# Reordering the statistics matmuls of one loop iteration on TensorE, in a fused LayerNorm, convolution and routing kernel

## The reference, cut to what matters

```python
x = x + conv(ln_c(x))          # ln_c: over the 64 channels; conv: group norm, 1x1 conv w1, relu, 1x1 conv w2, residual
t = tokens(x)                  # one token per pixel, 64 channels
t = t + ffn(ln_t(t))           # ffn: per image 32 experts choose 8 tokens each by a softmax of gate logits,
                               # expert MLP on the weighted sum of the 8, result added back to the 8 tokens
```

## Time and profile before

| what | us |
|---|---|
| median of 3 runs (lowest, highest) | 632.74 (632.73, 635.37) |
| time of the profiled execution | 639.6 |
| span of its trace | 637.9 |
| TensorE matmul busy | 535.4 |
| VectorE busy | 487.2 |
| ScalarE busy | 435.3 |

### The profile page before, as it was taken

One profiled execution on the slowest core, in us unless ns is written; L12 is line 12 of the kernel. 1 busy time (PEld: TensorE's weight loads), 2 busy tenths in 40 slices (PEclk: granted clock), 3 DMA queues, 4 the chain that ended last, 5 costly groups with the idle time before them and its releaser, 6 DMA issues.

```text
span 637.9 us, 14170 instructions
## 1 busy us (share of the span) xinstructions
PE 535.4 (84%) x5732; PEld 270.3 (42%) x5732; DVE 487.2 (76%) x950; ACT 435.3 (68%) x651; POOL 189.6 (30%) x116
## 2 busy tenths in 40 slices
PE   2749999898998899889989899989887988876982
PEld 1324444444444344444444444444443433434762
DVE  5574556689888988898789878988888687799620
ACT  2463779677976797679767976797677855984110
POOL 1007435023502260217020802080207145121144
PEclk9955999999999999999999999999998998987595
DMA  8960144714471447244634454445401255430000
GB/s 195 195 144 0 68 133 142 188 68 133 133 199 67 134 133 191 76 133 134 168 98 134 115 160 123 133 101 165 133 35 67 76 182 154 146 100 5 6 15 19
DMA packets 26752, 73.38 MB, mean 115 GB/s; under 512 B 4152, under 2 KB 4152, under 8 KB 22592
## 3 DMA queue, kind: packets, MB, share of 16 engines
q1 hardware_dynamic: 25664, 71.44, 40.9%
q0 software_dynamic: 1024, 1.05, 0.6%
HBM read 38.40 MB, written 34.08 MB: 114 GB/s over the span
## 4 chain that ended last, share of the span: by engine, by line
PE 41%; DVE 30%; ACT 13%; issue 12%; DMA 2%; POOL 1%; SPq 0%; ACTq 0%; DVEq 0%; POOLq 0%
PE st L372 11%; ACT junk L801 7%; DVE xs L948 7%; PE cv L383 6%; PE cv L391 6%; PE tl L400 6%; PE bc L494 5%; DVE us L938 5%; DVE lg L936 3%; DVE top_i L1035 2%; ACT tok L766 2%; DVE us L940 2%; DVE cnd L1030 2%; DMA xs<-in_x 2%; PE tl L409 2%
## 5 line engine op out<-in xcount | busy, mean ns | idle before, releaser
L1426 POOL TENSOR_TENSOR xs<-xs,us 128x1024 f32<-128x1024 f32 x64 | 151.2, 2379 | 367.2 <-DVE xs L948 173.4
L948 DVE SCALAR_TENSOR_TENSOR xs<-cv,vecs,xs 128x1024 f32<-128x1024 f32 x64 | 82.1, 1282 | 47.8 <-PE cv L391 47.7
L794 ACT ACTIVATE sqc<-us 128x1024 f32<-128x1024 f32 x64 | 67.5, 1054 | 46.2 <-DVE us L938 45.4
L761 ACT ACTIVATE hid<-cv,b1n 128x1024 f32<-128x1024 f32 x64 | 71.2, 1113 | 36.5 <-PE cv L383 36.0
L938 DVE TENSOR_TENSOR us<-xs,bc 128x1024 f32<-128x1024 f32 x60 | 73.0, 1216 | 19.7 <-PE bc L494 19.3
L400 PEld LDWEIGHTS tl<-ident,xs 128*128 128x128 f32 x512 | 63.8, 195 | 53.9 <-issue 53.9
L372 PE MATMUL st<-xs,stat_w 128*32 128x256 f32 x1024 | 74.5, 413 | 10.5 <-DMA xs<-in_x 9.4
L801 ACT ACTIVATE junk<-us 128x1024 bf16<-128x1024 f32 x64 | 67.3, 1051 | 22.8 <-DVE gsum L940 22.1
L940 DVE CUSTOM_DVE_ANT_0 us<-us,bc 128x1024 f32<-128x1024 f32 x60 | 72.9, 1215 | 11.2 <-PE bc L494 9.9
L400 PE MATMUL tl<-ident,xs 128*128 128x128 f32 x512 | 76.4, 294 | 0.9 <-ACT lg L776 0.9
L409 PE MATMUL tl<-xs,gcen 128*32 128x256 f32 x1024 | 69.4, 389 | 8.0 <-ACT tok L766 7.9
(11 more groups left out here) (210 smaller groups left out, 652.4 us busy)
## 6 DMA issues: line engine op xcount, KB each, us to landing
xs<-in_x SPq DMA_DIRECT2D x64, 512.0 KB, 7.0
out_rows<-tok SPq DMA_DIRECT2D x64, 512.0 KB
us<-in_e_w SPq DMA_DIRECT2D x8, 260.0 KB
xs<-in_e_w SPq DMA_DIRECT2D x8, 256.0 KB
sqc<-out_rows,idx_all POOLq DMA_INDIRECT x16
out_rows<-sqc,idx_all POOLq DMA_INDIRECT x16, 2.1
vecs<-in_b SPq DMA_DIRECT2D x4, 0.2 KB, 14.0
gate_bias<-in_gate_b SPq DMA_DIRECT2D x4, 0.1 KB, 12.3
```

The source lines that it names most:

```text
L948: nc.vector.scalar_tensor_tensor(out=xu, in0=cv[:], scalar=vecs[:, 3:4], in1=xu, op0=ALU.add, op1=ALU.add).then_inc(x1_done, 1)
L1426: nc.gpsimd.tensor_tensor(xu, xu, su, ALU.add).then_inc(s_done, 1)
```

## The change

In the loop TensorE issues four of its sums at other places. Nothing else is touched: no engine but TensorE has another order, and no instruction is added or taken away. In step 0 the square sums of the last group of the image before stand behind `conv2` and the spread `(0, 1)`. In step 2 `x1_sums` of group 0 stands behind `conv2`, the spread `(2, 1)` and the logits. In step 6 `x1_sums` of group 2 stands behind `conv2` and the spread `(6, 1)`. `x1_square_sums` of group 1 (units 2 and 3), in step 5 ahead of `conv2` until now, goes to step 4: in iterations 0 to 5 between the logits and the spread `(4, 1)`, in iterations 6 and 7 ahead of `(4, 2)`.

```diff
                 if s == 0 and b >= 0:
                     x1_sums(b, b % 2, NG - 1)
-                    x1_square_sums(b, NG - 1)
...
-                if s in (2, 4, 6):
-                    x1_sums(it, par, s // 2 - 1)
-                if s in (3, 5, 7):
+                if s == 4:
+                    x1_sums(it, par, 1)
+                if s in (3, 7):
                     x1_square_sums(it, (s - 3) // 2)
...
                     spread_at(it, (s, 1))
+                if s == 0 and b >= 0:
+                    x1_square_sums(b, NG - 1)
+                if s == 6:
+                    x1_sums(it, par, 2)
                 if b >= 0:
                     logits(b, b % 2, u)
+                if s == 2:
+                    x1_sums(it, par, 0)
+                if s == 4 and n + 1 < NB:
+                    x1_square_sums(it, 1)
                 if s == 4:
                     spread_at(it, (s, 1))
...
                     x_sums(n + 1, s // 2 - 2)
+                if s == 4 and n + 1 >= NB:
+                    x1_square_sums(it, 1)
                 spread_at(it, (s, 2))
```

## The result

The changed kernel takes 653.7 us (median of 4 runs, 652.28 to 654.76) against 633.44 (4 runs, 632.73 to 635.37): a ratio of 1.0314, interval 1.0295 to 1.0332, so 3.1% slower, about 20 us. The forecast was 645.9 with a range of 638.5 to 652.5. The direction and the mechanism were right; the loss is larger than the range allowed, by 1.2.

The account below looks back on a forecast made before the run. It saw TensorE and VectorE alternating in steps 0 to 4, ScalarE bounding relu(5) to relu(7). Orders and waits +6.25 plus clock 6.9 gave +13.2 on 632.74: 645.9 us, range 638.5 to 652.5.

Parts of the forecast that it names:

- The wait and its price: Step 4: TensorE idles 3.1 us for `square_x1(3)`, delaying S1 and relu(5); net loss 1.53 in iterations 1 to 5.
- Steps 0 and 2: Moved sums gain 0.20 in step 0 and 0.86 in step 2, together 1.06 an iteration.
- Steps 5 and 6 worth nothing: Steps 5 and 6: `conv2` and `x1` come about 1 earlier, but ScalarE's work covers them; costed at nothing.
- The clock: Behind the step 4 wait: falls to 1.2 GHz in nearly every one of iterations 0 to 5, 1.15 each, 6.9 in all.
- a fall does not last through all of it: Reason for pricing a fall at 1.15, between 0.63 (`conv1` alone hit) and about 2 (all work behind the wait hit).
- Iteration 0: S1 2.2 late, relu(5) 1.7, some 0.8 regained in step 5: +1.0 (bounds +0.5 and +1.7), before the clock term.
- Iterations 6 and 7: Gains where S1 stays ahead of the sums and waits for `conv2` shorten: -1.4 in iteration 6, -1.0 in iteration 7.
- The way from the profiled execution to the median: Plain runs lie 6.9 below the profiled 639.6, with the same loop, so +13.2 was added to 632.74.
- a second fall in each iteration: Rival "more falls": thinner step 5 brings a second fall, slowing `conv1(6)`; 6 x 1.2 more, 653 us, chance 0.07.

Follow-up runs that it names:

- the run with TensorE kept at work: Changed kernel plus three more groups of sums (24 matmul calls, results unused) ahead of the waiting square sums in step 4, iterations 0 to 5: 643.81 us, ratio 1.0171.
- the swap on ScalarE: Changed kernel with `square_x1(3)` put ahead of the square of S job 0 on ScalarE in step 4: 628.97 us, ratio 0.9915.
- the run without the step 4 part: Changed kernel with the square sums of units 2 and 3 left in step 5 ahead of `conv2`: 630.37 us, ratio 0.9933.
- the second trace: Kernel before, unchanged, profiled once more: 633.31 us, ratio 0.9998; its profiled execution has a span of 631.0.
- the two kernels where this fall is absent: Changed kernel with `square_x1(3)` ahead on ScalarE (628.97 us), and the same plus 8 zero-weight matmul calls in step 5 of iterations 0 to 5 (625.64 us).
- the step 2 part alone: Kernel before with only `x1_sums` of group 0 moved behind the logits in step 2: 629.64 us, ratio 0.9952.
- the square sums behind S1: Changed kernel with the square sums of units 2 and 3 behind S1 and `x_sums` in every iteration: 633.32 us, ratio 0.9994.

## Why the forecast missed: point by point

**The wait and its price: right.** An idle of 3.1 was forecast and 3.03 came; the iteration without a fall was forecast at 66.73 and measured at 66.71 to 66.74 (the run with TensorE kept at work). Where the wait comes from is shown by the swap on ScalarE, that it is the whole loss by the run without the step 4 part.

**Steps 0 and 2: right.** 0.20 and 0.86 forecast, 0.21 and 0.87 measured, 1.06 together and 64.10 for the iteration.

**Steps 5 and 6 worth nothing: right for iterations 1 to 5.** 64.1 with the square sums of step 5 ahead of `conv2` or behind it, and steps 0 and 2 alone account for the way from 65.19 to 64.10, which leaves nothing for step 6.

**The clock: right in kind, too small; the largest error.** A fall in each of iterations 0 to 5 was forecast, at 1.15 each, 6.9 in all. The falls came, and the short kind costs 1.14 here. But three of the six, in iterations 0, 2 and 4, were twice as long (6.83 us at the low clock instead of 3.41), and those of iterations 2 and 4 cost 1.92. The step that failed is the price behind the sentence "a fall does not last through all of it". Iterations 1 to 5 lost 15.0 against the second trace (2.66, 3.49, 2.69, 3.49, 2.71) where 5 x (1.53 + 1.15) = 13.4 was forecast: 1.6 missing. Iteration 0 lost 3.8 (65.34 against 61.58) where 1.0 + 1.15 = 2.2 was forecast. An estimate divides it: in the run with TensorE kept at work iteration 0 is 1.2 late when its step 6 begins, before that run's own fall, so the wait costs some 1.3 and the fall some 2.4. The falls together come to some 9.8, against 6.9.

**Iterations 6 and 7: put at -2.4, measured -0.5; the second error.** Iteration 6 was put at -1.4 and gained 0.3 (66.82 against 67.10). The prediction had S2 0.3 earlier than before. In step 4 of that iteration the square sums, which now stand ahead of S2, wait for ScalarE, and the clock falls:

```profile
499.40 1.45 PE L372 MATMUL st<-sqx,stat_w 128*32 128x256 f32 x16 [1.63 <-ACT sqx L790]
500.77 0.79 PE L494 MATMUL bc<-rstd_s,spread 32*128 32x256 f32 x4
501.49 1.99 PE L383 MATMUL cv<-us,w1n 64*64 64x512 f32 x8
```

Counted from the start of the iteration, S2 comes 0.1 later than in the second trace (43.95 against 43.84), and `conv1(5)` 0.4 later (44.67 against 44.27). Steps 5 to 7 give back 0.7 of the 1.1 that was forecast for them. In the two kernels where this fall is absent, both with the swap on ScalarE, the iteration takes 64.5. Iteration 7 was put at -1.0 and gained 0.2 (54.57 against 54.76). The gain in its steps 0 and 1 came as forecast (0.6), but its step 2 became 0.55 longer (6.74 against 6.19), a term that the prediction left out; the step 2 part alone gives the same 6.74. Step 6 brought 0.2.

**The way from the profiled execution to the median: a wrong premise that did little harm.** The prediction said that the plain runs lie 6.9 lower "and the same loop runs in them". The same loop didn't: 3.1 of those 6.9 us were the disturbed iteration 7. The forecast was added to the median, so this doesn't enter the sum.

**The rest.** Iterations 0 to 7 account for 15.0 + 3.8 - 0.3 - 0.2 = 18.3, where 13.2 was forecast. With that alone the time would be some 651, inside the range. Between the two spans (653.0 and 631.0) lie 22.0. The other 3.7 lie ahead of the loop (51.1 against 49.1) and behind it (74.8 against 73.1), in code that the change doesn't touch. These two stretches scatter over all traces here, 49.0 to 52.0 and 72.9 to 74.8, whichever kernel runs. Part of the 3.7 is the choice of executions: the profiled one of the changed kernel was 1.1 above its median, that of the second trace 0.6 below its own. The last 2 us of the 20.3 between the medians stay open: whether scatter or the changed loop brings them about was not settled.

**The range: too narrow.** Its upper end of 652.5 took a second fall in each iteration as a rare case (0.07), and neither falls of the long kind nor scatter of the ends was in it.

## What to carry to other kernels

Before an instruction is moved up in an in-order queue, find the end of what it waits for on the other engine, and then price not its own delay but that of the first thing queued behind it that another engine needs. Here 3 us of waiting ahead of a spread cost 2.6 an iteration, and 0.6 of waiting behind the same spread 0.8. In this kernel TensorE's clock was part of the price, of a gain too: filling one idle of 0.88 with useless matmuls gave back 0.8 an iteration. And take two profiles before one is read as the kernel's: a stall that only one of them has is not a term of the sum.

## What the runs showed of the hardware

The low clock came behind a single idle of 3.02 or 3.03 in iterations 1 to 5 of the changed kernel, of 2.46 in iteration 0 and of 1.63 in iteration 6. It also came, in some iterations and not in others of the same kernel, behind idles of 0.89 and 0.83 (without the step 4 part) or of 0.88 and 0.39 (the swap on ScalarE), separated by a little work. In iterations 0 to 6 of the changed kernel the low level lasted 3.41 or 6.83 us at a time, with TensorE busy nearly all of it, and in iterations 0 to 5 long and short falls alternated at an otherwise equal order. No run here shows what decides between the two. The price of a short one went from an estimated 0.6 (iteration 1 with the square sums behind S1) over 0.8 (the swap) and 1.14 (the changed kernel) to 1.5 (iteration 4 without the step 4 part).

The Trainium skill (TensorE: Matmul & The Clock Gate, Part 1) puts the ramp penalty, for modelling, below 1% of a typical kernel's span. As a ceiling on what the clock can cost this does not hold here: holding TensorE at work through the wait took some 10 us off, 1.5% of the time. The Trainium skill's section on HAM oscillation, on the same page, describes a loop in which TensorE waits in each pass and starts each time at the low clock. The changed kernel agrees with it in iterations 0 to 6, with one fall in each.
